# Head of the gate scan: four row groups projected side by side, VectorE shares the gates of the first unit, bf16 remainders made by TensorE in PSUM

## The reference, cut to what matters

```python
x = conv1x1(x, W_in)                       # 48 -> 96 channels
x = depthwise_conv3x3(x, W_dw) + b_dw      # "x3" in the kernel
x_proxy = conv1x1(x, W_xd)                 # 96 -> 16 channels, "px"
ws, Ls, Us, Ds = (conv1x1(x_proxy, W) for W in (W_w, W_l, W_u, W_d))
xs = stack(x, x^T, flip(x), flip(x^T))     # four directions d
Gl, Gm, Gr = split(ws);  s = |Gl| + |Gm| + |Gr| + eps
Gl, Gm, Gr = Gl / s, Gm / s, Gr / s
# along W, in chunks of 8 columns, from h = 0:
h = Ls * xs + Gl * up(h) + Gm * h + Gr * down(h)
y = sum over d of w_m[d] * (h * Us + xs * Ds)
out = conv1x1(grn(layernorm(y)), W_out)
```

## Time and profile before

| | us |
|---|---|
| median of 3 runs | 1041.44 (1039.17 to 1043.06) |
| the profiled execution: its time | 1044.38 |
| the profiled execution: its span | 1042.6 |
| TensorE busy in it | 844.8 (81%) |
| VectorE busy | 803.5 (77%) |
| ScalarE busy | 571.1 (55%) |
| POOL busy | 248.4 (24%) |

### The profile page before, as it was taken

One profiled execution on the slowest core, in us unless ns is written; L12 is line 12 of the kernel. 1 busy time (PEld: TensorE's weight loads), 2 busy tenths in 40 slices (PEclk: granted clock), 3 DMA queues, 4 the chain that ended last, 5 costly groups with the idle time before them and its releaser, 6 DMA issues.

```text
span 1042.6 us, 20791 instructions
## 1 busy us (share of the span) xinstructions
PE 844.8 (81%) x8172; PEld 577.6 (55%) x8172; DVE 803.5 (77%) x2016; ACT 571.1 (55%) x853; POOL 248.4 (24%) x276
## 2 busy tenths in 40 slices
PE   4799999999999999999999979795976753363534
PEld 2577887877787778878777754561221210031222
DVE  8688888888888888888888854745228999988852
ACT  2276767776767766677666633325347553555102
POOL 6122222222222222222222212741111212124301
PEclk9799999999999999999999979887877556565656
DMA  8000000000000000020000001000024665566300
GB/s 249 25 2 2 2 2 2 2 2 2 2 2 2 2 2 2 2 90 9 3 2 2 1 2 46 1 0 1 1 39 83 122 122 114 98 122 116 65 17 15
DMA packets 12200, 35.73 MB, mean 34 GB/s; under 512 B 1943, under 2 KB 4423, under 8 KB 11847
## 3 DMA queue, kind: packets, MB, share of 16 engines
q0 software_dynamic: 6480, 22.81, 11.6%
q1 hardware_dynamic: 5623, 11.60, 3.6%
HBM read 10.81 MB, written 0.79 MB: 11 GB/s over the span
## 4 chain that ended last, share of the span: by engine, by line
PE 62%; DVE 24%; issue 5%; ACT 4%; POOL 2%; DMA 2%; POOLq 0%; SPq 0%; DVEq 0%; ACTq 0%
PE narrow L1424 5%; PE wide L1347 4%; PE scores_a L1396 4%; PE scores_b L1396 4%; PE last L1501 4%; PE scores_a L1383 3%; DVE prod L983 3%; PE scores_b L1407 3%; PE scores_b L1383 3%; PE scores_a L1407 3%; DVE prod L991 3%; PE narrow L1443 3%; PE narrow L1454 3%; PE last L1497 2%; PE wide L1487 2%
## 5 line engine op out<-in xcount | busy, mean ns | idle before, releaser
L374 POOL TENSOR_TENSOR stb<-stb,neg_half 128x4 f32<-128x4 f32 x48 | 48.4, 1007 | 265.7 <-DVE stb L678 265.7
L1099 ACT ACTIVATE d<-d 128x768 f32<-128x768 f32 x96 | 80.6, 839 | 17.9 <-DVE d L625 17.4
L1424 PEld LDWEIGHTS narrow<-v,pt 128*64 128x64 f32 x2304 | 79.7, 139 | 13.4 <-issue 13.4
L1424 PE MATMUL narrow<-v,pt 128*64 128x54 f32 x2304 | 86.0, 226 | 0.1
L369 POOL TENSOR_TENSOR sta<-sta,neg_half 128x4 f32<-128x4 f32 x48 | 48.8, 1017 | 116.8 <-DVE sta L565 116.8
L1106 ACT ACTIVATE pt<-scores_a 128x768 f32<-128x768 f32 x48 | 38.9, 810 | 56.7 <-PE scores_a L1407 56.7
L606 DVE COPY v<-narrow 64x96 f32<-64x96 f32 x192 | 49.0, 255 | 18.8 <-PE narrow L1359 13.8
L1671 PE MATMUL scores_b<-xb,gates_w 128*32 128x512 bf16 x192 | 27.0, 571 | 43.9 <-DVE yo L1008 38.2
L1115 ACT ACT_TABLE_LOAD x47 | 60.3, 1283 | 0.8
L1099 ACT ACT_TABLE_LOAD x46 | 59.0, 1283 | 0.8
L612 DVE TENSOR_REDUCE mx<-scores_a 128x12 f32<-128x768 f32 x48 | 46.0, 957 | 17.1 <-PE scores_a L1396 17.1
(11 more groups left out here) (312 smaller groups left out, 2289.2 us busy)
## 6 DMA issues: line engine op xcount, KB each, us to landing
gsum<-mag POOLq DMA_DIRECT2D x16, 512.0 KB, 4.8
ysum<-yo POOLq DMA_DIRECT2D x7, 768.0 KB, 5.8
ysum<-xd POOLq DMA_DIRECT2D x6, 768.0 KB, 5.9
gsum<-mag POOLq DMA_DIRECT2D x16, 256.0 KB, 4.7
wts<-in_wpack SPq DMA_DIRECT2D x6, 442.0 KB, 6.3
sed_w<-in_sed_in SPq DMA_DIRECT2D x1, 2304.0 KB, 8.1
graw<-in_gates_in SPq DMA_DIRECT2D x1, 1152.0 KB, 5.2
x_all<-in_x_tok SPq DMA_DIRECT2D x8, 96.0 KB, 2.9
```

The lines of the kernel that those rows point to most:

```text
L1099: act.activation(d, d, ACT.Exp).then_inc(p_ready[u], 1)
L1424: op = pe.matmul(y_ps[64 * b:64 * b + 64, q * VO:(q + 1) * VO], t.pt[:, q, h, 64 * b:64 * b + 64], t.v[:, q, b, h * VO:(h + 1) * VO], star ...
```

## The change

Four things are done, all in the last layer's head.

1. `conv3` takes one or two m. For a pair, the ky = 2 slice of one reads rows 0 to 47 of the maps and that of the other rows 64 to 111 (the same image lines in the moved copy, with ky = 1), in turn in one stream. The weights stand in both halves for that (last lines of the diff). conv3(3, 4) and conv3(5) move behind the gates of units 1 and 2, and the `take_x3` of them behind `take_gates` of units 1 and 2.
2. `project_px` takes several c and goes through them inside each g, so that consecutive matmuls are in different row groups, with a bank for each c.
3. The remainders are made in PSUM: after ScalarE has rounded the high part, TensorE adds minus (a negative identity, bf16) times it to the same bank; the middle part is copied out (for c < 4 by VectorE, later by ScalarE), TensorE takes it off rows 96 to 127, and ScalarE copies the low part out. `split_px` is gone from VectorE, in unit 2 too. Projections of 4, 5 stand behind out_gates(2), those of 6, 7 between in_gates(3) and all of gates(4).
4. In unit 0, VectorE makes the copies of k = 1, 2 and adds mag to gsum; POOL's four DMAs for it go. Semaphore counts are shifted to fit. A 128 x 2560 fp32 tensor is laid between others in the first layers' memory and used by nobody.

```diff
+PX_BANK = (4, 5, 6, 7, 6, 7, 6, 7)
...
+        l1("above_sums", [128, 2560])
```

On POOL:

```diff
-                        pool.wait_ge(gate_taken[1 + k], 3 * u + 2 + h)
+                        pool.wait_ge(gate_taken[1 + k], 3 * u - 1 + h)
                         if k:
-                            pool.wait_ge(sum_ready[h], 32 * u + 16)
+                            pool.wait_ge(sum_ready[h], 32 * u - 16)
                         accumulate(gsum[u % 2][:, lo:hi], mag[k][:, lo:hi], sum_ready[h])
-            magnitudes(0)
             for u in range(8):
```

On VectorE:

```diff
+            step(dve.tensor_scalar(minus[:], ident[:], -1.0, None, ALU.mult))
...
-            def split_px(e):
-                px, r = B8[(4 if e < 4 else 6) + e % 2], rest3[e % 2]
-                dve.wait_ge(px_hi, e + 1)
-                dve.tensor_tensor(r, px[:], xb[:, e, :], ALU.subtract).then_inc(px_left, 1)
-                dve.wait_ge(px_left, e + 1)
-                dve.tensor_copy(xb[32:64, e, :], r[32:64]).then_inc(xb_ready, 1)
-                step(dve.tensor_copy(mid3[96:128], r[96:128]))
-                dve.tensor_tensor(xb[96:128, e, :], r[96:128], mid3[96:128], ALU.subtract).then_inc(xb_ready, 1)
+            def middle_px(c):
+                dve.wait_ge(px_rest, c + 1)
+                dve.tensor_copy(xb[32:64, c, :], B8[PX_BANK[c]][32:64, :]).then_inc(xb_mid, 1)
+
+            def first_magnitudes():
+
+                for g in range(G):
+                    cols = slice(512 * g, 512 * (g + 1))
+                    for k in (1, 2):
+                        dve.wait_ge(first_abs, 2 * g + k)
+                        dve.tensor_copy(gate[0][:, k, cols], B8[k][:]).then_inc(first_copied, 1)
+                    for k in (1, 2):
+                        if k == 2:
+                            dve.wait_ge(first_added, 2 * g + 1)
+                        dve.tensor_tensor(gsum[0][:, cols], gsum[0][:, cols], mag[k - 1][:, cols], ALU.add).then_inc(first_added, 1)
...
+                if u == 0:
+                    first_magnitudes()
                 sums = gsum[u % 2]
...
-                if u == 2:
-                    split_px(4)
-                    split_px(5)
...
-                if u == 2:
-                    split_px(6)
-                    split_px(7)
...
             for c in range(4):
-                split_px(c)
+                middle_px(c)
```

On ScalarE:

```diff
-                    if u and k and g % 2 == 0:
-                        act.wait_ge(sum_ready[g // 2], 32 * u)
-                    act.activation((gsum[u % 2], mag[0], mag[1])[k][:, cols], B8[k][:], ACT.Abs)
-                    act.activation(gate[u % 2][:, k, cols], B8[k][:], ACT.Copy).then_inc(gate_taken[k], 1)
+                    if u == 1 and k and g == 0:
+                        act.wait_ge(first_added, 6)
+                    if u > 1 and k and g % 2 == 0:
+                        act.wait_ge(sum_ready[g // 2], 32 * (u - 1))
+                    op = act.activation((gsum[u % 2], mag[0], mag[1])[k][:, cols], B8[k][:], ACT.Abs)
+                    if u == 0 and k:
+                        op.then_inc(first_abs, 1)
+                    else:
+                        act.activation(gate[u % 2][:, k, cols], B8[k][:], ACT.Copy).then_inc(gate_taken[k], 1)
...
-                    act.wait_ge(sum_ready[h], 32 * u + 32)
+                    if u:
+                        act.wait_ge(sum_ready[h], 32 * u)
+                    else:
+                        act.wait_ge(first_added, (4, 6)[h])
...
+            def middle_px(c):
+                act.wait_ge(px_rest, c + 1)
+                act.activation(xb[32:64, c, :], B8[PX_BANK[c]][32:64, :], ACT.Copy).then_inc(xb_mid, 1)
+
+            def low_px(c):
+                act.wait_ge(px_last, c + 1)
+                act.activation(xb[96:128, c, :], B8[PX_BANK[c]][96:128, :], ACT.Copy).then_inc(xb_low, 1)
+
+            def split_px(cs):
+                for take in (round_px, middle_px, low_px):
+                    for c in cs:
+                        take(c)
...
-            for c in range(4):
-                round_px(c)
+            for take in (round_px, low_px):
+                for c in range(4):
+                    take(c)
             for g in range(G):
                 take_gates(0, g)
-            take_x3(3)
-            take_x3(4)
             first_guess(0)
...
             for u in range(1, 8):
+                if u == 4:
+                    split_px((6, 7))
                 if u >= 2:
                     act.wait_ge(lud_taken, 9 * (u - 2) + 7)
                 for g in range(G):
                     take_gates(u, g)
                 if u == 1:
+                    take_x3(3)
+                    take_x3(4)
+                if u == 2:
                     take_x3(5)
-                if u in (2, 3):
-                    round_px(2 * u)
-                    round_px(2 * u + 1)
+                if u == 3:
+                    split_px((4, 5))
```

On TensorE:

```diff
+            def conv3(*ms):
...
+                for part in range(2):
+                    for kx in range(3):
+                        for order in (ms, ) if part else [(m,) for m in ms]:
+                            for i in range(4):
+                                for m in order:
+                                    hb, g = m // 3, m % 3
+                                    j = 4 * (i % 2) + 2 * hb
+                                    if part == 0:
+                                        rows, ky, tap = slice(0, 64 + C), 0, kx
+                                    elif m == ms[0]:
+                                        rows, ky, tap = slice(0, C), 2, 3 + kx
+                                    else:
+                                        rows, ky, tap = slice(64, 64 + C), 1, 3 + kx
+                                    op = pe.matmul(B8[X3_BANK[m]][32 * i:32 * i + 32, :], taps_w[rows, tap, 32 * g:32 * g + 32],
+                                                   a3[i // 2][rows, j:j + 2, ky:ky + 16, kx:kx + 16],
+                                                   start=(kx == 0 and part == 0), stop=(kx == 2 and part == 1))
...
+            def project_px(cs):
+
+                for c in cs:
+                    if c < 4:
+                        pe.wait_ge(x3_ready, 6)
+                    elif c < 6:
+                        pe.wait_ge(x3_ready, 12)
+                    else:
+                        pe.wait_ge(xb_low, c - 1)
                 for g in range(G):
+                    for c in cs:
+                        rows = slice(32 * (c % 4), 32 * (c % 4) + 32)
+                        op = pe.matmul(B8[PX_BANK[c]][:], l3w[rows, Q_XD + 128 * g:Q_XD + 128 * (g + 1)],
+                                       x3[rows, c // 4, 512 * g:512 * (g + 1)], start=(g == 0), stop=(g == G - 1))
+                        if g == G - 1:
+                            op.then_inc(px_done, 1)
+                for c in cs:
+                    pe.wait_ge(px_hi, c + 1)
+                    pe.matmul(B8[PX_BANK[c]][:], minus[:], xb[:, c, :], start=False, stop=True, skip_group_check=True).then_inc(px_rest, 1)
+                for c in cs:
+                    pe.wait_ge(xb_mid, c + 1)
+                    pe.matmul(B8[PX_BANK[c]][96:128, :], minus[32:64, 32:64], xb[32:64, c, :], start=False, stop=True,
+                              skip_group_check=True).then_inc(px_last, 1)
...
-            for m in range(3):
-                conv3(m)
-            project_px(0)
-            project_px(1)
-            conv3(3)
-            project_px(2)
-            project_px(3)
+            conv3(0, 1)
+            conv3(2)
+            project_px(range(4))
             gates(0)
-            conv3(4)
-            gates(1, (0,))
             for u in range(8):
                 in_gates(u)
+                if u == 0:
+                    gates(1, (0,))
                 if u >= 5:
                     tail(0, ((0,), (3,), (5,))[u - 5])
-                if u < 7:
+                if u < 7 and u != 3:
                     gates(u + 1, (1, 2))
                 if u in (5, 6):
                     tail(0, (1,) if u == 5 else (4,))
                 if u == 0:
+                    conv3(3, 4)
+                if u == 1:
                     conv3(5)
-                if u in (1, 2):
-                    project_px(2 * u + 2)
-                    project_px(2 * u + 3)
+                if u == 3:
+                    project_px((6, 7))
+                    gates(4)
                 out_gates(u)
-                if u < 6:
+                if u == 2:
+                    project_px((4, 5))
+                elif u < 6:
                     gates(u + 2, (0,))
...
-    taps[:C, 0:3], taps[64:, 0:3], taps[:C, 3:6] = dw[0], dw[1], dw[2]
+    taps[:C, 0:3], taps[64:, 0:3], taps[:C, 3:6], taps[64:, 3:6] = dw[0], dw[1], dw[2], dw[2]
```

More of the change, by code:

```diff
@@ L109, in build @@
         ident2 = sb("ident2", [128, 128], BF16)
+        minus = sb("minus", [128, 128], BF16)
         a2 = sb("a2", [64 + C, 8, PADW, PADW])
@@ L201, in build @@
         yq = sb("yq", [128, HB])
```

(54 more changed lines are left out.)

6 lines of the change are left out of this document (3 added, 3 removed).

## The result

The changed kernel takes 1012.76 us (median of 4 runs, 1012.30 to 1017.06) against 1040.44 for the kernel before in the same series (4 runs): a ratio of 0.974 with a 95% interval of 0.9706 to 0.9774, 27.7 us faster. Forecast were 1014.2 and 27.2 us. The profiled execution has a span of 1010.4 us (its time is 1012.31).

A forecast was written before the change was run, and what follows sets the result against it. The chain to the first scan step was taken as the bound, then VectorE. Gains 15.4 + 7.3 + 9.4, less 4.4, 0.3 and 0.2, make 27.2 us: 1014.2 against the median 1041.44, range 1007 to 1023.

The forecast's parts named there:

- The likeliest case: Whole kernel: the main forecast of 1014.2 us, given 59% for a time between 1011 and 1018 us.
- the wait in unit 4: Unit 4: late projection of chunks 6, 7 delays the gates and sum DMAs, so VectorE waits 4.4 us for the guess.
- Convolutions: First convolutions up to the projection: eight matmuls at once save three sets, 2.6 us, less 0.3 for form changes.
- Projection: Projections 0 to 3: 12 matmuls in three sets of four row groups take 2.9 us, bounds 2.6 and 8.
- Remainders: Split after the first projections, with TensorE subtracting in PSUM: 4.9 us; first gate matmul 15.4 us earlier in all.
- Gates to scan: First gate matmul to first scan step: VectorE sums replace DMAs, 17.1 us instead of 24.4, gain 7.3.
- Unit 2: Unit 2 loses the remainders of chunks 4 to 7 on VectorE: 33.2 to 23.8 us, gain 9.4.
- What comes late: Units 1 to 4: moved convolutions stay hidden, 1.1 us to spare before unit 1; chunks 6, 7 cost 4.4 us.
- Rival a): Unit 4: no wait, as projection of chunks 6, 7 gets full clock and the DMA chain is shorter; 1010 us, 15%.
- b): Unit 1: the new convolution pair comes late at half clock, VectorE waits 4 us; 1018 to 1021 us, 17%.
- c): Gates to scan: VectorE is no quicker at the sums than the DMAs; 1021.5 us, 6%.
- Rival d): Convolution pairs: the eight matmuls of a set do not run at once; up to 1049 us, slower than before, 3%.

The follow-up runs named there:

- after_again: The changed kernel unchanged, run again as yardstick on the same chip as a variant with earlier projections: 1013.4 us, ratio 0.9726 to the kernel before.
- dma_sums: The changed kernel with unit 0's sums made as before, by ScalarE copies and POOL's four accumulating DMAs: 1017.9 us.
- the first experiment: Three variants of the changed kernel: projections chunk by chunk (1022.1 us), ky = 2 slices of convolution pairs not in turn (1011.9), convolutions single (1017.1).
- no_alternation: The changed kernel with the ky = 2 slices of a convolution pair not in turn, four matmuls of one row half, then four of the other: 1011.9 us.
- chunk_order: The changed kernel with the 12 projections chunk by chunk instead of the four row groups in turn: 1022.1 us.

## Why the prediction was right

The likeliest case came: the three stages got shorter by the mechanisms that were named, the wait in unit 4 came where it was forecast, and all rivals failed. That the totals agree within 0.5 us is partly luck, since the errors of the terms cancel. Point by point:

1. **Convolutions.** 2.6 us less 0.3 for changes of form were forecast, and 2.5 came. Some 0.5 of this is the clock: the first six sets, which begin at its half level, took 1.8 us more than at the full one here and 2.3 before. (In after_again, with the half clock lasting longer, the stage takes 18.4 us.) The eight matmuls of a set do run at once, which was taken as granted from two rows. At the change to the 48-row form its first matmul starts 0.08 us before the last 112-row one has ended, as between projection and convolution before. The rows thus show a small price for a change of form, not that TensorE runs empty.
2. **Projection.** This term was mis-sized: 2.9 us were forecast and 4.5 came, since the clock was at half for its first 3 us. The forecast rested on a row that was misread: 2.78 us in the earlier trace rows are nine of the twelve passes, and projections 2 and 3 together took 3.81 us at the full clock, the second beginning about two passes behind the first (the row stands behind these points). Projections 0 and 1, with 5.61 us in the same rows, had met the half clock in their second part (from 749.5 on), so the half clock could have been reckoned with. Four row groups abreast were nevertheless as quick as hoped: from one pass of four to the next it took 0.43 us at the full clock (743.74 to 744.17) and 0.85 at half, as between passes of one alone. The Trainium skill (TensorE: Matmul & The Clock Gate, Measured speedup vs the span model) has 3.07 times for four row tiles; in this stream of passes it is four times, at either clock. **Remainders:** 4.9 forecast, 5.0 measured. Up to the gates the pair of profiles gives 13.5 us instead of 15.4; against the second profile of the kernel before it would be 15.0, because the old stage to the first gate matmul itself takes 20.6 or 22.3 by the clock it meets.
3. **Gates to scan.** Forecast 17.1, measured 16.8. Three groups took VectorE 7.66 us, 2.5 each as said, and it began 2.1 us after the first gate matmul. dma_sums confirms the cause, with 6.2 us for the DMAs instead of 7.3.
4. **Unit 2.** 9.4 us forecast; unit 2 went from 33.2 to 23.7, and VectorE's busy time in it from 32.5 to 23.6. No run put the remainders of chunks 4 to 7 alone back on VectorE.
5. **What comes late.** The step with the thinnest support was right. The guess of unit 1 ended at 786.03 with VectorE asking at 786.99: 1.0 us to spare, 1.1 forecast. The wait in unit 4 was 3.6 us for a forecast 4.4 (3.9 and 4.2 in the two other profiles of the changed kernel): ScalarE took the gates 12.5 us into unit 3 (13.3 forecast), and from the first sum DMA to the end of the guess it took 13.3 us (13.5). It is not paid twice: from the end of unit 4 to the end of the span it takes 128.1 us (from 882.3), where the kernel before took 128.7 (from 913.9).

The row of point 2, TensorE in the kernel before:

```profile
759.94 3.81 PE L1708 MATMUL wide<-x,l3w 32*128 32x512 f32 x12
```

Sum of what was measured in the first pair of profiles, from the first convolution on: 2.5 + 11.1 + 7.6 + 6.2 = 27.4 us, where 6.2 is 9.4 less 3.6, which makes 5.8, and 0.4 of small shifts that were not traced. Against the forecast of 27.2, the stages up to the first gate matmul gave 1.6 us less than 15.4 - 0.3; the gates to the scan gave 0.3 more, the wait was 0.8 shorter, and the rest is unit 2 (0.1 more by the windows), the small shifts, and the 0.2 us for the instruction that makes `minus`, which no run isolates. Rival a) failed in both its parts: the clock stayed at 0.50 during the projection of chunks 6, 7 (833 to 839), and the DMA chain with the guess took 13.3 us (13.5 in the kernel before). Rivals b) and c) failed by point 5 and point 3. Rival d) fell twice over: the eight run at once, and without alternating too. That was not needed for the forecast, but my reason in the first experiment, that standing next to each other is what lets them run together, was wrong for the convolutions; for the projections the order does matter.

## What to carry to other kernels

Where VectorE is the bound of a long loop, a subtraction of a bf16 part can be had from TensorE in PSUM with a negative identity. It is worth it in the serial head too if several chunks go through the chain abreast (9.5 us here, against 14.7 with VectorE's subtractions and 15.6 chunk by chunk). Put TensorE work that waits for another engine in pieces: its first part where TensorE is idle, its waiting part behind whatever the bound engine asks for next; moved as one block it only moved the wait from unit 4 to unit 2. And compare a stage from landmarks of its own: two profiles of one kernel differed by 5 us ahead of the edit, and by 1.7 us in one stage by the clock that it met. A row of a chain that counts fewer passes than the work has is not the time of that work; look for all of them in the timeline.

## What was not expected of the hardware

Row groups overlap by themselves across a block of four matmuls at four column groups (0.03 us apart in no_alternation), but not across a block of three matmuls on one row group (1.9 us apart in chunk_order, or 2.2 passes). What part of TensorE makes the difference is open. And the head's projections met a half clock (0.53 from 740.0 to 743.4) 1.9 us after a stretch of 15 us in which TensorE was never idle; in the kernel before they began at the full clock (1.00 from 747.58 to 749) and fell to half at about 749.5:

```profile
740.00:743.40 3.40, 3.06 (x16) 1.68 (x20) 0.00 (x0) 0.09 (x1) 0.00 (x0) 0.53 0.00 0
743.40:750.00 6.60, 4.01 (x23) 1.07 (x23) 2.48 (x4) 4.11 (x8) 0.00 (x0) 0.99 0.00 0
```
